# Attention 0 of a gated cross-attention block: the softmax sums divide the context in row form instead of in feature-major form

## The chip, the cores and the metric

The kernel runs on one core of one Trainium2 chip. The metric is the device time of one execution in microseconds (us). The names of the engines in the profile: PE is TensorE (PEld are its weight loads), DVE is VectorE, ACT is ScalarE, POOL is GpSimd, SP is SyncE, which here issues nearly all DMA transfers. SBUF is the on-chip memory, PSUM the matmul results' memory in 8 banks.

## The reference

The block adds four residual parts to x (8 batches of 100 tokens of 512 features); the change is in the first.

```python
x = x + jnp.tanh(g_xattn[0]) * _L0_xattn_ref(_layernorm(x, axis=-1), ctx_1024, ctx_1024, mask, Wq, bq, Wk, bk, Wv, bv)
x = x + jnp.tanh(g_ffn[0]) * _L0_ffn_ref(_layernorm(x, axis=-1), ...)
x = x + jnp.tanh(g_xattn[1]) * _L1_xattn_ref(_layernorm(x, axis=-1), ctx_1024, ctx_1024, ..., Wo, bo)
x = x + jnp.tanh(g_ffn[1]) * _L1_ffn_ref(_layernorm(x, axis=-1), ...)
```

Attention 0 has 16 heads of 32 features over 722 keys per batch:

```python
q = _heads(x_q @ Wq.T + bq)
k = _heads(x_k @ Wk.T + bk)
v = _heads(x_v @ Wv.T + bv)
scores = jnp.einsum('bhqw,bhkw->bhqk', q, k) / np.sqrt(W).astype(np.float32)
scores = scores - 10000.0 * (1.0 - m)
p = jax.nn.softmax(scores, axis=-1)
h = jnp.einsum('bhqk,bhkw->bhqw', p, v)
```

Since the weights of a softmax add up to one, the bias of V may be added after the division by the sums.

## The kernel before

Every engine has its own instruction stream, written out by hand, and engines wait for one another by semaphores. Large products are done as three products of rounded halves (high times high, high times low, low times high), so most tiles exist as a pair h and l (`cxh`, `cxl`, `wkh`, ...).

An attention runs over 64 **pairs** of heads (8 batches, 8 pairs each, loop variable `i`, batch `b = i // 8`). In pair i TensorE computes the scores of pair i+1 (L926 to L931), turns the exponentials of pair i with an identity matrix (L942), does one or two **jobs**, which project keys (L864) or values (L868) of the next batch, and multiplies pair i-1's weights with V (`weigh`, L964; in the last batch L957). ScalarE does the exponentials (L1955) and the high halves, VectorE the maxima (`peak`, L1386), the low halves of the turned weights (`low_turned`, L1392), the gathering of the context (`low_weighed`, L1407 and L1411, in the last batch L1402) and the low halves of the jobs (`low_job`, L1366 for keys, L1370 for values).

The results of jobs, of `weigh` and of the steps below go to two PSUM banks in turn, the **ring**. The list `RINGS` gives the order, and `ring_free(item)` makes TensorE wait until the item two places earlier has been read: `v_job` for a job (DVE's low half), `v_fin` for a `weigh` (the context gathered), `v_sc` for "inv", `v_x0` for "res". So a late VectorE reaches TensorE through these four.

After the 8 pairs of batch b the context stands feature-major in `QT` (512 features x 100 tokens), not yet divided. Then, in pairs of the next batch:

- near i%8 = 2: `inverse` (DVE, L1420) takes the reciprocals `rr` of the sums (100 x 16), `spread_sums` (POOL, L2341) copies each to 32 columns of `rx` (100 x 512);
- i%8 = 4 (`scaled_at`; pairs 12, 20, ..., 60): `turn_sums` (PE, L973, four transposes) turns `rx`, `scale_out` (DVE, L1429) multiplies `QT` with it, `add_bias` (ACT, L1988, four activations) adds the V bias as a column;
- i%8 = 6 (`out_at`; pairs 14, 22, ..., 54, and 61): `turn_out` (PE, L993, four transposes) turns `QT` to rows, `add_out` (DVE, L1492) adds it times tanh(g) to x, which SP has loaded to `x0`. Its semaphore is `v_x0`. Statistics, root and normalized rows follow for the first feed-forward part.

Batch 7 does the same behind the last pair: there the bias is added as a row (`row`, L2567 and L2570 on POOL), and TensorE goes on with the products of the feed-forward part's units 0 and 1 (`inputs`, L1237) in between. VectorE takes a pair's `low_weighed` ahead of its maxima in pairs marked `early`.

## Time and profile before

| | |
|---|---|
| timed runs, median of 3 | 1575.21 us (1574.67 to 1576.0) |
| span of the profiled execution, first to last instruction | 1573.8 us |
| median of the timed runs less that span | 1.4 us |
| PE busy | 1562.0 us, 99% |
| DVE, ACT, POOL busy | 65%, 62%, 27% |
| granted TensorE clock | 1.000 |

The profile is of one execution; its own whole time isn't recorded apart from its span. Attention 0's pairs lie between about 60 us and 485 us, the first feed-forward part follows up to about 1005 us, then attention 1 and the second feed-forward part. Times on the trace are us from the span's start. A bracket at the end of a row, as [0.26 <-ACT V L1921], says how long the engine stood idle before it and who ended that.

### The profile page before, as it was taken

To read this page: it belongs to the slowest core of one execution; us is meant where nothing else is said; L and a number is where in the kernel's file an instruction comes from.
4 is the path that set the end of the run, shared out by engine and by line. 5 is a ranking of instruction groups with operands and counts; after the bars stand their busy time and mean duration, and the time that the engine had idled before them with its cause. 6 is when DMAs were issued, how large, how long until landed. Compare 5 with 4: busy or idle time off the path is not lost.

```text
span 1573.8 us, 25733 instructions
## 1 busy us (share of the span) xinstructions
PE 1562.0 (99%) x9306; PEld 1428.1 (91%) x9306; DVE 1025.1 (65%) x1814; ACT 972.5 (62%) x2014; POOL 426.0 (27%) x570
## 2 busy tenths in 40 slices
PE   9999999999999999999999999999999999999999
PEld 7999899999989999999999998889999989988765
DVE  6577887787786562123644425637777777778987
ACT  5676777677775455444544435447677767767676
POOL 4221222222145222222322222311211121123741
PEclk9999999999999999999999999999999999999999
DMA  8766767687582225554365642576676677658500
GB/s 246 190 169 167 200 179 198 160 206 182 137 220 98 95 81 201 185 180 165 106 230 192 214 165 93 179 181 184 160 193 175 169 189 179 171 142 225 193 13 31
DMA packets 149974, 261.29 MB, mean 166 GB/s; under 512 B 41136, under 2 KB 94000, under 8 KB 149709
## 3 DMA queue, kind: packets, MB, share of 16 engines
q1 hardware_dynamic: 149505, 259.24, 58.8%
q8 instruction: 85, 1.39, 0.4%
q14 instruction: 52, 0.43, 0.1%
q10 hardware_dynamic: 332, 0.23, 0.1%
HBM read 191.01 MB, written 58.57 MB: 159 GB/s over the span
## 4 chain that ended last, share of the span: by engine, by line
PE 94%; DVE 3%; ACT 2%; issue 1%; DMA 0%; ACTq 0%; DVEq 0%
PE ps L1237 33%; PE ps L864 16%; PE ps L868 14%; PE ps L964 8%; PE ps L942 8%; PE ps L1171 2%; PE ps L1033 2%; PE ps L884 2%; PE ps L931 2%; PE ps L926 2%; PE ps L1188 1%; PE ps L929 1%; PE ps L930 1%; ACT P L1955 1%; PE ps L1082 1%
## 5 line engine op out<-in xcount | busy, mean ns | idle before, releaser
L1237 PE MATMUL ps<-ah_f,wh_f 128*128 128x400 f32 x1288 | 442.0, 344 | 0.0
L1237 PE MATMUL ps<-al_f,wh_f 128*128 128x400 f32 x1288 | 441.3, 343 | 0.0
L2319 POOL TENSOR_TENSOR cxl<-raw,cxh 128x384 fp32r<-128x384 f32 (+1 forms) x112 | 105.7, 965 | 556.9 <-ACT cxh L1897 556.9
L1819 DVE TENSOR_TENSOR wl_f<-raw_f,wh_f 128x1024 fp32r<-128x1024 f32 x85 | 103.7, 1223 | 232.2 <-POOL wh_f L2309 232.2
L1386 DVE TENSOR_REDUCE nmax<-ps 100x1 f32<-100x722 f32 x256 | 220.8, 903 | 33.2 <-PE ps L930 29.6
L1237 PEld LDWEIGHTS ps<-al_f,wh_f 128*128 128x128 f32 x1288 | 242.2, 188 | 0.0
L1237 PEld LDWEIGHTS ps<-ah_f,wh_f 128*128 128x128 f32 x1288 | 241.9, 188 | 0.1
L1955 ACT ACTIVATE P<-ps,nmax 100x722 f32<-100x722 f32 x256 | 220.4, 864 | 27.4 <-DVE nmax L1386 27.2
L1967 ACT ACTIVATE PT<-ps 128x400 fp32r<-128x400 f32 x384 | 165.9, 505 | 70.3 <-PE ps L942 69.2
L2237 ACT ACTIVATE raw_f<-wl_f 128x1024 f32<-128x1024 f32 x88 | 93.4, 1062 | 173.7 <-DVE wl_f L1819 173.6
L1392 DVE TENSOR_TENSOR PT<-ps,PT 128x400 fp32r<-128x400 f32 x384 | 196.3, 566 | 3.2
L2309 POOL CAST wh_f<-raw_f 128x1024 fp32r<-128x1024 f32 x85 | 92.8, 1092 | 334.0 <-PE ps L1237 328.3
L864 PE MATMUL ps<-cxh,wkh 128*128 128x338 f32 (+1 forms) x512 | 174.9, 342 | 0.7 <-DVE cxl L1356 0.7
L864 PE MATMUL ps<-cxh,wkl 128*128 128x338 f32 (+1 forms) x512 | 168.4, 329 | 0.0
L864 PE MATMUL ps<-cxl,wkh 128*128 128x338 f32 (+1 forms) x512 | 167.5, 327 | 0.0
L942 PE MATMUL ps<-ident,P 100*128 100x100 f32 (+1 forms) x1536 | 152.9, 249 | 0.7 <-ACT P L1955 0.7
L942 PEld LDWEIGHTS ps<-ident,P 100*128 100x128 f32 (+1 forms) x1536 | 143.1, 137 | 11.1 <-ACT P L1955 0.9
L964 PE MATMUL ps<-PT,V 128*128 128x400 f32 x720 | 152.1, 346 | 0.6 <-DVE QT L1411 0.6
L964 PEld LDWEIGHTS ps<-PT,V 128*128 128x128 f32 x720 | 129.7, 188 | 7.1 <-DVE V L1378 3.7
L1366 DVE SCALAR_TENSOR_TENSOR ksl<-ps,cols,ksh 128x338 fp32r<-128x338 f32 (+1 forms) x120 | 70.8, 590 | 95.9 <-ACT ksh L1908 95.9
L868 PE MATMUL ps<-wvh,cxh 128*128 128x512 f32 x320 | 131.7, 411 | 0.9 <-DVE V L1366 0.9
L868 PE MATMUL ps<-wvh,cxl 128*128 128x512 f32 x320 | 126.0, 394 | 0.0
(227 smaller groups left out, 2669.0 us busy)
## 6 DMA issues: line engine op xcount, KB each, us to landing
KS<-kd SPq DMA_DIRECT2D x192, 361.0 KB
raw_f<-in_h SPq DMA_DIRECT2D x64, 512.0 KB, 4.2
raw_f<-in_gud SPq DMA_DIRECT2D x48, 512.0 KB, 4.3
raw<-in_ctx SPq DMA_DIRECT2D x64, 192.0 KB, 3.5
raw_f<-in_w SPq DMA_DIRECT2D x24, 512.0 KB, 3.5
kd<-ksh SPq DMA_DIRECT2D x60, 192.0 KB, 2.2
kd<-ksl SPq DMA_DIRECT2D x60, 192.0 KB, 2.5
raw<-in_ctx SPq DMA_DIRECT2D x64, 169.0 KB, 4.4
```

The costliest lines, as they stand in the source:

```text
L864: ins = e.matmul(o, m.wk[x][:, k, 128 * j[2]:128 * j[2] + 128], m.cx[y][:, k, off:off + n], start=(k == 0 and c == 0), stop=(k == 3 and c ...
L868: ins = e.matmul(o, m.cx[y][:, k, 128 * kt:128 * kt + KM[kt]], m.wv[x][:, k, :], start=(k == 0 and c == 0), stop=(k == 3 and c == 2))
L942: ins = e.transpose(ps[0:KM[kt], bank, o:o + S], m.P[0:S, (2 * i + h) % 3, 128 * kt:128 * kt + KM[kt]], ident[0:S, 0:S])
L964: ins = e.matmul(o, m.V[b % 2][0:r, kt, g, 128 * pr:128 * pr + 128], m.PT[0:r, i % 2, :, kt, :], start=(kt == 0), stop=(kt == KT - 1))
L1237: return e.matmul(o, p, q, start=start, stop=stop)
L1386: e.tensor_reduce(m.nmax[0:S, c:c + 1], scores_of(n), AX.X, ALU.max, negate=True).then_inc(v_max, 1)
L1392: e.tensor_tensor(lo, ps[:, bank, 0:400].rearrange("p (k n) -> p k n", k=2), raw32(hi), ALU.subtract).then_inc(v_t, 1)
L1819: e.tensor_tensor(wl[:, z, :], raw[:, r, :], raw32(wh[:, z, :]), ALU.subtract).then_inc(v_ul, 1)
L1955: e.activation(m.P[0:S, n % 3, :], scores_of(n), ACT.Exp, bias=m.nmax[0:S, c:c + 1], accum_out=m.rs[0:S, r:r + 1]).then_inc(a_exp, 1)
L1967: e.activation(m.PT[:, i % 2, 0, 2 * x:2 * x + 2, :], ps[:, bank, 0:400].rearrange("p (k n) -> p k n", k=2), ACT.Copy).then_inc(a_t, 1)
L2237: e.activation(raw[:, r, :], raw32(wl[:, z, :]), ACT.Abs, accum_out=low[:, z, 0:1]).then_inc(a_raw, 1)
L2319: e.tensor_tensor(m.cx[1][:, k, off:off + n], m.raw[:, k, off:off + n], raw32(m.cx[0][:, k, off:off + n]), ALU.subtract).then_inc(g_cx, 1)
```

## The change

In attention 0 alone the reciprocal sums are no longer spread, turned and multiplied into `QT`. The undivided context is turned to rows, and VectorE multiplies the rows in their PSUM bank with the reciprocals `rr`, 100 x 16 read with stride 0 over 32 columns; behind a wait for its own result the old L1492 follows. The V bias is loaded once as a row in pair 4, multiplied by tanh(g) on POOL in pair 8, and added to each batch's x rows by POOL (`add_row`) before DVE's sum. The "inv" items leave ring 0, and pairs 12, 20, ..., 60 are no longer `early`.

```diff
-        if scaled_at(_i) is not None:
+        if _l and scaled_at(_i) is not None:
             RINGS[_l].append(("inv", scaled_at(_i)))
...
-        row = at("row", PLACE[0]["Qs"], [128, D])[0:S, :]
+        row = rooms[0].rx[0:S, :, :].rearrange("p h j -> p (h j)")
...
-                        w.wait_ge(d_qs[1], qs_done(L, B - 1))
+                    if L == 0 and i == 4:
+                        w.wait_ge(d_row, 16 * 6)
                         e.dma_start(row, t["bv0"].partition_broadcast(S)).then_inc(d_row, 16)
...
                 def turn_out(b):
-                    if b < B - 1:
-                        w.wait_ge(a_fin, 4 * b + 4)
-                    else:
-                        w.wait_ge(v_sc, B)
+                    w.wait_ge(v_fin, 16 * b + 16)
+                    if summed(L, 8 * b + 7):
+                        w.wait_ge(a_pv, 8 * b + 8)
...
-                    turn_sums(B - 1)
                     add_low()
                     turn_normal(KEPT)
-                    inputs(0, 0, HN, 0, g_xf, 4, [0])
                     turn_out(B - 1)
-                    inputs(0, 0, HN, 0, g_xf, 4, [1])
+                    inputs(0, 0, HN, 0, g_xf, 4)
...
                 def add_out(b):
                     w.wait_ge(a_g, 1)
-                    w.wait_ge(d_x, 16 * (b + 1))
+                    w.wait_ge(g_row, b + 1)
                     w.wait_ge(p_res, b + 1)
+                    w.wait_ge(v_inv, b + 1)
                     x = rows_in(b)
+                    o = ps[0:S, ring_bank(L, ("res", b)), :].rearrange("p (h j) -> p h j", h=H)
+                    me.then(e.tensor_tensor(o, o, m.rr[0:S, :].unsqueeze(2).to_broadcast([S, H, W]), ALU.mult))
+                    me.settle()
                     e.scalar_tensor_tensor(x, ps[0:S, ring_bank(L, ("res", b)), :], G["x0"][0:S], x, ALU.mult,
                                            ALU.add).then_inc(v_x0, 1)
...
-                    if scaled_at(i) is not None:
+                    if L and scaled_at(i) is not None:
                         add_bias(scaled_at(i))
...
+                def add_row(b):
+                    w.wait_ge(d_x, 16 * (b + 1))
+                    e.tensor_tensor(rows_in(b), rows_in(b), row, ALU.add).then_inc(g_row, 1)
...
-                    if scaled_at(i + 1) is not None:
+                    if L and scaled_at(i + 1) is not None:
                         spread_sums(scaled_at(i + 1))
+                    if L == 0 and i == 8:
+                        w.wait_ge(d_row, 16 * 7)
+                        w.wait_ge(a_g, 1)
+                        me.then(e.tensor_scalar(row, row, G["x0"][0:S], None, ALU.mult))
+                        me.settle()
+                    if L == 0 and out_at(i + 1) is not None:
+                        add_row(out_at(i + 1))
```

On TensorE in pair 12, between the turned exponentials (L942) and the first key job, and at the start of the second job (`wkh`, 128x384), the difference reads so; in brackets the semaphores that an instruction waits for:

```order
-L973 MATMUL ps<-ident,rx_54 128x100 [waits v_job,g_rx]
-L973 MATMUL ps<-ident,rx_54 128x100 x3
-L864 MATMUL ps<-cxh_49,wkh_58 128x338 [waits g_cx,v_fin]
+L864 MATMUL ps<-cxh_49,wkh_58 128x338 [waits g_cx,v_job]
...
-L864 MATMUL ps<-cxh_49,wkh_58 128x384 [waits v_sc]
+L864 MATMUL ps<-cxh_49,wkh_58 128x384 [waits v_fin]
```

The four transposes are gone, and the second job waits for the gathered context of pair 10 instead of for `scale_out`.

On VectorE the same pairs 14 and 15 (from `add_out` to the value job of pair 15) read so in the changed kernel; its lines are L1492 for the new product, L1494 for the old sum, L1389 for `low_turned`, L1367 for a value job's low half, L1383 for the maxima, L1404 and L1408 for the gathering:

```order
L1492 TENSOR_TENSOR ps<-ps,rr_55 100x512 [waits v_inv,p_res,g_row]
L1494 SCALAR_TENSOR_TENSOR x_108<-ps,gt,x_108 100x512 [waits v_self]
L1389 TENSOR_TENSOR PT_64<-ps,PT_64 128x2x200 [waits a_t] x3
L1367 TENSOR_TENSOR V_0_61<-ps,V_0_61 128x4x128 [waits a_job]
L1499 BN_STATS st<-x_108 100x6 [waits v_x0]
L1501 BN_AGGR mv<-st 100x2 [waits v_self]
L1383 TENSOR_REDUCE nmax_57<-ps 100x1 [waits a_exp,p_sc] x2
L1404 TENSOR_TENSOR sum_65<-ps,sum_65 64x200 [waits a_pv]
L1408 TENSOR_TENSOR QT_68<-ps,sum_65 32x100 [waits v_self]
L1408 TENSOR_TENSOR QT_68<-ps,sum_65 32x100
L1389 TENSOR_TENSOR PT_64<-ps,PT_64 128x2x200 [waits a_t] x3
L1367 TENSOR_TENSOR V_0_61<-ps,V_0_61 128x4x128 [waits a_job]
```

Before, the first two rows were the single L1492, with waits for `p_res` and `d_x`, and the other ten stood in the same order. In pair 12 VectorE has lost L1429 and does the two maxima ahead of the gathering, which stood before them.

## Rows read from the trace of the kernel before

**Rows 1.** The page: busy time of the engines, and the chain by engine

```profile
PE 1562.0 (99%) x9306; PEld 1428.1 (91%) x9306; DVE 1025.1 (65%) x1814; ACT 972.5 (62%) x2014; POOL 426.0 (27%) x570
...
PE 94%; DVE 3%; ACT 2%; issue 1%; DMA 0%; ACTq 0%; DVEq 0%
```

**Rows 2.** Waits of PE, 80 to 485 us: total, times, longest

```profile
PE ps L929 <- ACT P L1955: 1.3, 4, 0.4
...
```

**Rows 3.** Timeline of PE, pair 12, then pair 56: start, duration, what

```profile
142.46 1.20 PE L942 MATMUL ps<-ident,P 100*128 100x100 f32 x12
143.49 0.51 PE L973 MATMUL ps<-ident,rx 100*128 100x100 f32 x4
143.78 0.40 PE L864 MATMUL ps<-cxh,wkh 128*128 128x338 f32 x1
...
449.96 1.19 PE L942 MATMUL ps<-ident,P 100*128 100x100 f32 x12
450.93 0.40 PE L864 MATMUL ps<-cxh,wkh 128*128 128x338 f32 x1
```

**Rows 4.** The chain in order of time: key jobs of pairs 12 and 13

```profile
144.00 4.11 PE ps L864 x24
150.88 4.00 PE ps L864 x24
```

**Rows 5.** Timeline, pair 12: DVE's scale_out, PE's weight loads of both jobs

```profile
145.10 0.57 DVE L1429 TENSOR_TENSOR QT<-ps,QT 128x400 f32<-128x400 f32 x1
...
145.43 0.19 PEld L864 LDWEIGHTS ps<-cxh,wkl 128*128 128x128 f32 x1
145.73 0.19 PEld L864 LDWEIGHTS ps<-cxh,wkh 128*128 128x128 f32 x1
```

**Rows 6.** Timeline, pairs 14 and 15: DVE, and the weight load behind them

```profile
159.12 0.75 DVE L1492 SCALAR_TENSOR_TENSOR x<-ps,gt,x 100x512 f32<-100x512 f32 x1
...
161.57 0.69 DVE L1370 TENSOR_TENSOR V<-ps,V 128x512 fp32r<-128x512 f32 x1 [0.26 <-ACT V L1921]
162.18 0.68 DVE L1497 BATCH_NORM_STATS2 st<-x 100x6 f32<-100x512 f32 x1
...
167.17 0.69 DVE L1370 TENSOR_TENSOR V<-ps,V 128x512 fp32r<-128x512 f32 x1
...
168.03 1.07 PEld L964 LDWEIGHTS ps<-PT,V 128*128 128x128 f32 x6
```

**Rows 7.** Timeline of DVE, pair 12: two operations with a wait for itself between

```profile
142.37 0.36 DVE L1407 TENSOR_TENSOR sum<-ps,sum 64x200 f32<-64x200 f32 x1 [0.22 <-ACT sum L1982]
142.76 0.55 DVE L1411 TENSOR_TENSOR QT<-ps,sum 32x100 f32<-32x100 f32 x2
```

**Rows 8.** Timeline, pairs 60 to 62: ACT, PE, DVE

```profile
471.43 1.18 ACT L1988 ACTIVATE QT<-QT,cols 128x100 f32<-128x100 f32 x4
...
472.91 1.30 ACT L1967 ACTIVATE PT<-ps 128x400 fp32r<-128x400 f32 x3
...
472.12 1.19 PE L942 MATMUL ps<-ident,P 100*128 100x100 f32 x12
...
473.86 0.75 DVE L1492 SCALAR_TENSOR_TENSOR x<-ps,gt,x 100x512 f32<-100x512 f32 x1
...
476.42 1.73 DVE L1386 TENSOR_REDUCE nmax<-ps 100x1 f32<-100x722 f32 x2 [0.36 <-PE ps L930]
...
478.18 0.87 ACT L1955 ACTIVATE P<-ps,nmax 100x722 f32<-100x722 f32 x1
```

**Rows 9.** Timeline, end of attention 0: PE and DVE

```profile
484.49 0.51 PE L973 MATMUL ps<-ident,rx 100*128 100x100 f32 x4
...
484.92 0.19 PE L982 MATMUL ps<-low_f,magic 128*1 128x3 f32 x2
...
483.82 0.79 DVE L1520 TENSOR_SCALAR x<-x,mv,rq 100x512 f32<-100x512 f32 x1 [0.51 <-POOL rq L2424]
```

**Rows 10.** The line L2570: durations in ns, least, median, most

```profile
L2570 POOL TENSOR_TENSOR x<-x,row x1: 1300/1300/1300, 486.1 to 486.1; 100x512 f32<-100x512 f32 x1
```

More of the change, by code:

```diff
@@ L178 @@
             RINGS[_l].append(("pv", _i - 1))
-for _l in range(2):
-    RINGS[_l].append(("inv", B - 1))
+RINGS[1].append(("inv", B - 1))
 RINGS[0] += [("res", B - 1), ("xn", B - 1)]
@@ L898, in ring_free @@
                     elif old[0] == "inv":
-                        w.wait_ge(v_sc, B * L + old[1] + 1)
+                        w.wait_ge(v_sc, old[1] + 1)
                     elif old[0] == "out":
@@ L981, in add_low @@
                     w.wait_ge(v_const, 4)
[L982 removed]
+                    e.matmul(ps[0:1, 4, 400:403], magic[:, 2:3], low[:, 0:3, 0], start=True,
                              stop=True).then_inc(p_low, 1)
                 def turn_out(b):
[L987 to L990 removed]
+                    w.wait_ge(v_fin, 16 * b + 16)
+                    if summed(L, 8 * b + 7):
+                        w.wait_ge(a_pv, 8 * b + 8)
                     ring_free(("res", b))
@@ L1179, in down @@
                     w.wait_ge(d_wb[4 + q], 16)
-                    w.wait_ge(v_sc, 2 * B)
+                    w.wait_ge(v_sc, B)
                     if n == TILES - 2:
@@ L1417, in inverse @@
                     w.wait_ge(a_exp, LAST * L + 16 * b + 16)
-                    w.wait_ge(g_rx, B * L + b)
+                    if L:
+                        w.wait_ge(g_rx, b)
+                    else:
+                        w.wait_ge(v_x0, b)
                     z = b % 2
@@ L1433, in copy_low @@
                     w.wait_ge(p_low, 1)
-                    e.tensor_copy(low[0:1, 0:3, 1], ps[0:1, ring_bank(L, ("inv", B - 1)), 400:403]).then_inc(v_low, 1)
+                    e.tensor_copy(low[0:1, 0:3, 1], ps[0:1, 4, 400:403]).then_inc(v_low, 1)
                 def add_projected(n):
@@ L1648, in attention @@
                 for i in range(NP + 1):
-                    early = scaled_at(i) is not None or L == 0 and i < NP - 7 and (
+                    early = L and scaled_at(i) is not None or L == 0 and i < NP - 7 and (
                         out_at(i) is not None or turned_at(i) is not None) or L == 0 and NP - 7 < i < NP - 2
@@ L1675, in attention @@
                         add_out(out_at(i))
-                    if scaled_at(i) is not None:
+                    if L and scaled_at(i) is not None:
                         scale_out(scaled_at(i))
@@ L1708, in attention @@
                     copy_low()
-                    scale_out(B - 1)
                     low_normal(KEPT)
-                    w.wait_ge(g_row, 1)
                     add_out(B - 1)
@@ L1984, in add_bias @@
                 def add_bias(b):
-                    w.wait_ge(v_sc, B * L + b + 1)
+                    w.wait_ge(v_sc, b + 1)
                     for g in range(4):
@@ L2139, in attention @@
                         high_q(b + 1)
-                    if scaled_at(i) is not None:
+                    if L and scaled_at(i) is not None:
                         add_bias(scaled_at(i))
@@ L2562, in attention @@
                         tile_roots(2)
-                spread_sums(B - 1)
                 if L == 0:
-                    w.wait_ge(d_row, 16 * 7)
-                    w.wait_ge(a_g, 1)
-                    me.then(e.tensor_scalar(row, row, G["x0"][0:S], None, ALU.mult))
-                    me.settle()
-                    w.wait_ge(d_x, 16 * B)
-                    e.tensor_tensor(x7, x7, row, ALU.add).then_inc(g_row, 1)
+                    add_row(B - 1)
                     high_unit(3)
```

12 lines of the change are left out of this document (5 added, 7 removed).

## The prediction

> **What bounds the kernel now.** I read the page first: TensorE is busy 99% of the span and holds 94% of the chain that ended last [rows 1]. So only what TensorE does less, or waits more or less for, counts. Its waits over attention 0 [rows 2] show the second thing: in 405 us its scores are held by exponentials four times, 1.3 us in all, and these fall in the last batch, which has no projection jobs to fill TensorE. So there are two regimes: batches 1 to 6 of the pair loop, bound by TensorE, where VectorE and ScalarE matter only where their slack ends, and the last batch, bound by the loop scores, maxima, exponentials, turning. ScalarE's bias and POOL's spreading lie beside TensorE's work in the first.
>
> **What is taken off TensorE.** In pair 12 the turned exponentials start at 142.46 and the first key job at 143.78, so 1.32 us later; in pair 56, where no L973 stands between, it is 450.93 - 449.96 = 0.97 [rows 3]. Four transposes cost 0.35 us, not the 0.51 of their row, which counts pipelined ends. Six batches (pairs 12 to 52) are in the first regime: 6 x 0.35 = 2.1 us.
>
> There is a second gain in the same pair. The second key job's first weight load starts at 145.73, 0.06 after `scale_out` ends (145.10 + 0.57), while the load before it came at 145.43 and loads there follow each other by about 0.16: so it was held by `v_sc`, some 0.14 late [rows 5]. The price is in the chain: the 24 key products of pair 12 took 4.11 us, those of pair 13 4.00 [rows 4], and all six batches repeat that (0.09 to 0.11). The changed job waits for pair 10's context instead. VectorE now gathers it behind its two maxima: these can take the gathering's place at about 142.4 [rows 7] and last 1.7 (1.73 in [rows 8]); the gathering adds 0.39 + 0.55 [rows 7], so it is ready near 145.1, while the job, with 0.35 less before it, loads near 145.43 + 0.16 - 0.35 = 145.24. That is close, but in time. Gain 0.10 a batch, so 0.45 with the transposes.
>
> **What is added to VectorE, and how it reaches TensorE.** The new product over 100x512 in PSUM has no row. The nearest is L1370, a tensor_tensor from PSUM over 512 columns, 0.69 us [rows 6]; reading `rr` with stride 0 I price at nothing, writing to PSUM in place of SBUF too. Then comes the wait for its own result: L1411 starts 0.39 after an L1407 of 0.36 [rows 7], so 0.03 on top, and I take 0.72 to 0.73 in all. The bounds: below 0.61, the start-to-start time behind L1370 with no wait (162.18 - 161.57, [rows 6]); above 1.30, POOL's own sum over the same 100x512 [rows 10], far off and on another engine. I take the near row.
>
> Where does this lateness go? In pair 14 VectorE goes straight from `add_out` (159.12) through `low_turned` to the value job's low half at 161.57, where it had stood idle for 0.26 [rows 6]. So 0.47 of the 0.73 remain. From there to the low half of pair 15's value job at 167.17 no row of VectorE has an idle bracket, so that starts near 167.64 and ends at 168.33. Who waits for it? By the ring, `weigh` of pair 14 takes the bank of that job, two places earlier, and its first weight load was issued at 168.03, when the old end, 167.86, was just past [rows 6]. With 0.06 for the semaphore [rows 5] the load now comes at 168.39, 0.36 late. Of a late load TensorE's queue absorbs a little: in pair 12 0.14 late cost 0.10. So 0.36 less 0.05, about 0.31 us per batch. The other two places on that road, `weigh` of pair 13 behind `v_x0` and pair 15's key job behind `v_fin`, come late by less than this, and lateness at an earlier place isn't paid twice.
>
> Net per batch: -0.35 - 0.10 + 0.31 = -0.14; six batches -0.84 us. The TensorE saving is nearly given back by a VectorE that had 0.1 us of slack.
>
> Here a rule of the Trainium skill can be weighed. The rows show that without a wait the next operation starts 0.08 before the end of the 0.69 us one, and with a wait for itself 0.03 behind the end [rows 6, 7], so the wait costs about 0.11. The Trainium skill, "VectorE: DVE Perf Modes", section "The DRAIN you can't avoid", says that a semaphore after each operation costs nothing extra. By it the product would take 0.61, the stall 0.19 instead of 0.31, and the six batches would give -1.56 instead of -0.84. The trace doesn't agree with the rule for these short operations, and I go by the trace.
>
> **Pairs 60 to 64.** ScalarE is on the loop here. L1988's four activations (1.18 from 471.43) stood in front of L1967 at 472.91; without them it can follow TensorE's L942 (472.12 plus a third of its 1.19, and a little) at about 472.66: -0.25 [rows 8]. L973 of pair 60 is free, since TensorE waits behind it. But one pair on, `add_out` of batch 6 stands between the maxima and `low_turned`: +0.73 against an idle time of 0.36, so the maxima of pair 62 start at 476.79 and end at 478.52, and the exponential that started at 478.18 starts 0.34 later, the 0.25 already spent [rows 8]. The rest of the loop, the statistics of batch 6 and POOL's root, on which normalized rows at 483.82 wait [rows 9], all move by that 0.34.
>
> At the very end L973 goes, which holds TensorE from 484.49 to 484.92 [rows 9], 0.43, but the transposes of `turn_out` now stand ahead of the products of unit 0 and wait for the last gathered context, on VectorE behind the normalized rows (483.82 + 0.79 + 0.34 = 484.95, [rows 9]); before, products covered that. Unhindered, TensorE would stand there at about 484.92 + 0.34 - 0.43 = 484.83 plus 0.4 for the four transposes of the normalized rows, so at 485.2; the context is gathered by 484.95 + 0.26 and some 0.2 of semaphores, 485.4 (0.26 an estimate from the halves of L1411, [rows 7]). That exposes 0.2. Sum of the tail: +0.34 - 0.43 + 0.2 = +0.1, with bounds of -0.4 (nothing late) and +0.6 (a dear product).
>
> **Edits at nothing.** POOL is busy 27% [rows 1]: eight sums of 1.30 for eight copies, in pairs where it waits for ScalarE; without that cover the sum stands ahead of its context splits. The x rows are loaded two pairs ahead. In pair 60 the sum stands ahead of two weight splits and may bring the root of batch 6 some tenths late, which I count within the 0.34 above. SP's one load only moves from pair 58 to pair 4. Behind 500 us nothing changes.
>
> **Sum.** 1573.8 - 0.84 + 0.1 = 1573.1 for the span; the median of the runs shown is 1.4 above it, so 1574.5 us.
>
> **The rivals.** *The stalls stay hidden* (17%): the value job's low half can slip because the load at 168.03 didn't really need it, or the product is cheap. Then all six 0.45 and the tail's 0.4 stay: -3.1, 1572.1 us. For it speaks that no row shows TensorE waiting there; against it that the old end was only 0.17 before the load. *The product is dear* (12%), the other side: reading and writing one bank costs VectorE 1.30. The stall per batch becomes 0.92, net +0.47, six times +2.8, and the tail adds 0.6: 1578.6 us. It decides from a product of 0.83 on, where 0.45 is used up; past 1.25 the loss can be measured. *The wait is free*, the page's rule worked out as a mechanism of these rows (8%): -1.56 and +0.1, 1573.7 us. *The moved gathering is late* (5%): pair 12's second job finds `v_fin` later than its load near 145.25, each 0.1 late costs 0.1, six times; with 0.3 late -0.84 becomes +0.96, so 1576.3 us. The forecast has 58%.
>
> **Chances and range.** A measurement of this kernel can tell about 0.2%, 3.15 us, from no change. Beyond it on the fast side lies half of the first rival, 8%; on the slow side most of the second, 9%; the rest, 83%, is within. The range 1572.2 to 1576.8 takes in most of the first rival, the third and fourth, and leaves out the dear product.
>
> **What the changed profile would show.** L973 with 32 products fewer, no L1429 and L1988 before 500 us. The product's own row near 0.69, L1494 0.72 behind its start. Key products of pair 12 at 4.00 in the chain. The weight load of `weigh` in pair 15 directly behind the value job's low half, about 0.06 after its end, six times; if it follows the last key load in step instead, the first rival holds. The distance from pair 12 to pair 20 on TensorE shorter by 0.14. Between 475 and 479 us VectorE without an idle bracket. Wrong would make it: a product of over 0.83, or a wait of TensorE at a job or turning that I counted as in time.

## The result, and the profile of the changed kernel

The change made the kernel slower: 1581.0 us (median of 5 runs, 1580.7 to 1585.6) against 1574.9 us (5 runs, 1574.7 to 1576.0), a ratio of 1.0046 with a 95% interval of 1.0034 to 1.0057. The quotient of the two medians is 1.0039; the ratio is larger, and two of the five runs lie at 1583.9 and 1585.6. The profiled execution spans 1579.0 us, where before's spanned 1573.8. That lies outside the range of the forecast.

The page, busy time and chain, as in [rows 1]:

```profile
PE 1560.1 (99%) x9274; PEld 1425.2 (90%) x9274; DVE 1026.0 (65%) x1814; ACT 965.1 (61%) x1986; POOL 428.6 (27%) x569
PE 93%; DVE 3%; DMA 2%; POOL 1%; ACT 1%; issue 1%; SPq 0%; DVEq 0%; ACTq 0%
```

TensorE has its 32 products fewer and 1.9 us less work, and yet the span is longer. The new thing in the chain is DMA, 2%. The waits of PE, 60 to 500 us, beside [rows 2] (engine, line, what it waited for: us in total, times, longest):

```profile
PE ps L942 <- ACT P L1955: 2.4, 1, 2.4
PE ps L1007 <- DVE x L1522: 2.2, 1, 2.2
PE ps L942 <- DVE PT L1389: 1.6, 1, 1.6
PE ps L929 <- ACT P L1955: 1.0, 3, 0.4
PE ps L957 <- DVE QT L1408: 0.8, 1, 0.8
```

Before, beside the row in [rows 2]:

```profile
PE ps L942 <- ACT P L1955: 0.7, 1, 0.7
PE ps L957 <- DVE QT L1411: 0.4, 1, 0.4
```

Three waits, 6.2 us in all, each once, stand where only 0.7 us stood. The timeline shows where: all are in the last two pairs of batch 7 and behind them.

```profile
476.53 1.52 PE L942 MATMUL ps<-ident,P 100*128 100x100 f32 x12 [1.57 <-DVE PT L1389]
...
482.09 2.26 PE L942 MATMUL ps<-ident,P 100*128 100x100 f32 x12 [2.36 <-ACT P L1955]
484.05 4.18 PE L957 MATMUL ps<-PT,V 128*64 128x200 f32 x36
488.16 0.19 PE L982 MATMUL ps<-low_f,magic 128*1 128x3 f32 x2
490.56 0.57 PE L1007 MATMUL ps<-ident,x 100*128 100x100 f32 x4 [2.22 <-DVE x L1522]
...
491.32 0.43 PE L1234 MATMUL ps<-ah_f,wh_f 128*128 128x400 f32 x1
```

Following them back leads to POOL, which executes in order. Its timeline (in brackets the idle time ahead of a row and what ended it):

```profile
461.31 1.04 POOL L2463 CAST wh_f<-raw_f 128x1024 fp32r<-128x1024 f32 x1 [8.27 <-DMA raw_f<-in_w]
...
466.93 1.04 POOL L2457 TENSOR_TENSOR al_f<-QT,ah_f 128x400 fp32r<-128x400 f32 x1
473.20 1.28 POOL L2346 TENSOR_TENSOR x<-x,rx 100x512 f32<-100x512 f32 x1 [5.23 <-DMA x<-in_x]
474.43 1.03 POOL L2463 CAST wh_f<-raw_f 128x1024 fp32r<-128x1024 f32 x1
475.54 2.36 POOL L2465 TENSOR_TENSOR wl_f<-raw_f,wh_f 128x1024 fp32r<-128x1024 f32 x1
...
486.14 0.23 POOL L2417 TENSOR_SCALAR rq<-mv 100x1 f32<-100x1 f32 x1
```

At 467.97 POOL comes to `add_row` of batch 6 and stands there for 5.23 us, because the x rows have not landed. Before, the same load was awaited by VectorE alone, at 473.86 [rows 8], with no visible wait. Now the split of weight tile 1 (L2463, L2465) stands behind it, and the root of batch 6 behind that. The same two in before's timeline of POOL:

```profile
468.80 1.04 POOL L2458 CAST wh_f<-raw_f 128x1024 fp32r<-128x1024 f32 x1
...
480.90 0.22 POOL L2412 TENSOR_SCALAR rq<-mv 100x1 f32<-100x1 f32 x1 [0.39 <-DVE mv L1499]
```

The other seven of POOL's eight sums found their rows landed: none has a bracket in the timeline. The chain, in order of time, has the load itself:

```profile
462.43 10.70 DMA x<-in_x
473.20 1.28 POOL x L2346
```

10.70 us for 200 KB. Two weight tiles of 512 KB each were requested from 461.48 on, and the load right behind them, 0.95 us later. The other engines, ACT and DVE:

```profile
477.93 1.06 ACT L2237 ACTIVATE raw_f<-wl_f 128x1024 f32<-128x1024 f32 x1 [3.68 <-POOL wl_f L2465]
...
474.51 0.70 DVE L1492 TENSOR_TENSOR ps<-ps,rr 100x512 f32<-100x512 f32 x1 [2.10 <-POOL x L2346]
...
489.05 1.46 DVE L1522 TENSOR_SCALAR x<-x,mv,rq 100x512 f32<-100x512 f32 x1 [2.12 <-POOL rq L2429]
```

So one wait reaches TensorE three times: through VectorE's late product (1.57), through ScalarE, which sums the magnitudes of the late weight tile's low half (L2237) ahead of its exponentials (2.36), and through the late root (2.22).

There is a further loss that no wait shows. Twelve turnings and the products behind them took 1.03 us and 3.43 us start to start before (from L942 over L957 to L973 at 484.49 [rows 9]):

```profile
480.03 1.25 PE L942 MATMUL ps<-ident,P 100*128 100x100 f32 x12 [0.72 <-ACT P L1955]
481.06 3.59 PE L957 MATMUL ps<-PT,V 128*64 128x200 f32 x36
```

Now they take 484.05 - 482.09 = 1.96 and 488.16 - 484.05 = 4.11, so 1.6 us more. The windows, with the granted clock in the third column from the end, then DMA's share and GB/s:

```profile
460.00:465.00 5.00, 4.70 (x47) 4.17 (x45) 4.50 (x10) 4.14 (x10) 3.61 (x3) 1.00 1.04 287
465.00:470.00 5.00, 4.50 (x40) 3.60 (x37) 4.30 (x9) 5.00 (x14) 2.80 (x4) 1.00 1.02 293
...
480.00:485.00 5.00, 2.91 (x18) 2.92 (x19) 3.78 (x10) 3.90 (x10) 4.77 (x5) 0.70 0.00 0
```

Behind idle TensorE the granted clock was 0.70 on average over these 5 us, where before it was 1.00. In windows of 1 us it is 0.52, 0.50 and 0.50 from 482 to 485 and 0.78 in the next: the lower level, 1.2 GHz, for some 3.4 us behind the wait of 2.36, and 2.4 GHz again. And from 455 on all sixteen DMA engines were busy (1.02 to 1.04): the load joined a full queue. In before's windows the share there is the same 1.03 to 1.05.

From `weigh` ahead of pair 57 (L964 at 451.09, before 452.89) to the first product of unit 0 (491.32, before 485.39 and 0.35 for the four L993 that then stood behind it) it is 40.2 us against 32.9, so 7.4 more. The three waits give 6.2 less the 0.7 that before waited for exponentials there, a longer wait of L957 0.4, the clock 1.6, and L973 is gone, -0.4: 7.1 together, within a few tenths of it. The batches ahead had won 1.6 us. The two together make 5.8, and the spans differ by 5.2; the other 0.6 lies outside these two stretches, 0.2 of it ahead of the first scores.

### The profile page after: what moved, and what is told of

Read it like the earlier page. It is cut to its first block, busy times and chain, and to the rows that moved or that the text cites. A ratio compares the mean times of both kernels' runs of the same rounds, so it can differ in the third digit from the quotient of the medians.

```text
span 1579.0 us, 25608 instructions
## 1 busy us (share of the span) xinstructions
PE 1560.1 (99%) x9274; PEld 1425.2 (90%) x9274; DVE 1026.0 (65%) x1814; ACT 965.1 (61%) x1986; POOL 428.6 (27%) x569
## 4 chain that ended last, share of the span: by engine, by line
PE 93%; DVE 3%; DMA 2%; POOL 1%; ACT 1%; issue 1%; SPq 0%; DVEq 0%; ACTq 0%
PE ps L1234 33%; PE ps L864 16%; PE ps L868 14%; PE ps L964 8%; PE ps L942 8%; PE ps L1168 2%; PE ps L1032 2%; PE ps L884 2%; PE ps L931 2%; PE ps L926 2%; PE ps L1185 1%; PE ps L930 1%; PE ps L929 1%; DMA x<-in_x 1%; DMA kd<-ksl 1%
## 5 line engine op out<-in xcount | busy, mean ns | idle before, releaser
L1383 DVE TENSOR_REDUCE nmax<-ps 100x1 f32<-100x722 f32 x256 | 220.8, 904 | 35.8 <-PE ps L930 32.9
L2237 ACT ACTIVATE raw_f<-wl_f 128x1024 f32<-128x1024 f32 x88 | 93.4, 1062 | 177.2 <-DVE wl_f L1819 173.5
L1389 DVE TENSOR_TENSOR PT<-ps,PT 128x400 fp32r<-128x400 f32 x384 | 196.8, 568 | 4.9 <-ACT PT L1967 1.5
L942 PE MATMUL ps<-ident,P 100*128 100x100 f32 (+1 forms) x1536 | 154.2, 250 | 3.9 <-ACT P L1955 2.4
L942 PEld LDWEIGHTS ps<-ident,P 100*128 100x128 f32 (+1 forms) x1536 | 143.9, 138 | 14.8 <-ACT P L1955 2.6
L964 PE MATMUL ps<-PT,V 128*128 128x400 f32 x720 | 152.8, 347 | 0.6 <-DVE QT L1408 0.6
L964 PEld LDWEIGHTS ps<-PT,V 128*128 128x128 f32 x720 | 129.0, 188 | 8.9 <-DVE V L1375 3.7
```

The source lines that it names most:

```text
L942: ins = e.transpose(ps[0:KM[kt], bank, o:o + S], m.P[0:S, (2 * i + h) % 3, 128 * kt:128 * kt + KM[kt]], ident[0:S, 0:S])
L964: ins = e.matmul(o, m.V[b % 2][0:r, kt, g, 128 * pr:128 * pr + 128], m.PT[0:r, i % 2, :, kt, :], start=(kt == 0), stop=(kt == KT - 1))
L1383: e.tensor_reduce(m.nmax[0:S, c:c + 1], scores_of(n), AX.X, ALU.max, negate=True).then_inc(v_max, 1)
L1389: e.tensor_tensor(lo, ps[:, bank, 0:400].rearrange("p (k n) -> p k n", k=2), raw32(hi), ALU.subtract).then_inc(v_t, 1)
L2237: e.activation(raw[:, r, :], raw32(wl[:, z, :]), ACT.Abs, accum_out=low[:, z, 0:1]).then_inc(a_raw, 1)
```

## The experiments

Times are medians of 6 to 11 runs (the change: 5). The ratio is to the kernel before on the same chip, with its 95% interval; before's median was 1574.9 beside the change and 1575.1 to 1575.3 beside the others. The single runs of one kernel spread over 2 to 5 us, so two medians that differ by less than about 1 us are not clear of the noise; where the text reads such a difference, it says so.

| run | us | ratio |
|---|---|---|
| the change | 1581.0 | 1.0046 [1.0034, 1.0057] |
| old_with_wait | 1580.6 | 1.0035 [1.0023, 1.0047] |
| no_row6 | 1575.9 | 1.0003 [0.9994, 1.0013] |
| x6_before_units | 1580.1 | 1.0029 [1.0019, 1.0040] |
| x6_no_product | 1579.4 | 1.0025 [1.0015, 1.0034] |
| x6_before_all | 1580.3 | 1.0030 [1.0019, 1.0041] |
| row7_apart | 1579.4 | 1.0027 [1.0016, 1.0037] |
| row6_behind | 1577.6 | 1.0014 [1.0005, 1.0023] |
| row6_after | 1575.4 | 1.0001 [0.9992, 1.0010] |
| x6_then_units | 1579.6 | 1.0026 [1.0015, 1.0036] |
| mended | 1576.1 | 1.0004 [0.9995, 1.0013] |
| mended_no_product | 1575.2 | 0.9999 [0.9990, 1.0008] |
| old_mended | 1577.1 | 1.0011 [1.0002, 1.0020] |
| mended_one_step | 1575.4 | 1.0003 [0.9994, 1.0012] |
| best | 1575.0 | 1.0000 [0.9991, 1.0009] |
| best_no_product | 1573.4 | 0.9989 [0.9980, 0.9998] |

**The wait alone, in the old kernel.**

```
+                    if L == 0 and i == 60:
+                        w.wait_ge(d_x, 16 * 7)
                     if L == 0 and i in (58, 60, 61):
                         prepare((i - 57) // 2)
```

> The kernel before the change, with a single addition: in pair 60 POOL waits for the transfer of batch 6's x rows before it splits the weights of unit 1. No instruction is added, moved or left out. Theory A: the wait alone reproduces the loss; POOL, which without it starts this split at 468.8 us, starts it near 473.2, and the time is 4 to 6 us above the 1574.9 of before: 1579 to 1581 us. Theory B (the added work, not the wait): within 0.5 us of before, 1574.4 to 1575.4 us.

1580.6 us. POOL waited until the rows landed, as in the changed kernel (timeline of POOL):

```profile
472.31 1.04 POOL L2458 CAST wh_f<-raw_f 128x1024 fp32r<-128x1024 f32 x1 [4.86 <-DMA x<-in_x]
```

A semaphore wait without any work, in a kernel that has none of the change, gives 5.2 of the 6.1 us. So the wait is shown as the cause. The road from POOL to TensorE is in part another one, though (PE):

```profile
487.55 0.56 PE L973 MATMUL ps<-ident,rx 100*128 100x100 f32 x4 [2.94 <-POOL rx L2341]
```

The spread sums of batch 7, late behind the split, hold the old kernel, where the normalized rows hold the changed one. The exponential of pair 63 is late in both (1.73 here, 2.36 there), and the granted clock is 0.50 behind the last wait here too, from 490 to 492.

**The sum of batch 6 left out.** VectorE waits for the rows itself, as before; batch 6 lacks the V bias.

```
-                    if L == 0 and out_at(i + 1) is not None:
+                    if L == 0 and out_at(i + 1) is not None and i < 56:
                         add_row(out_at(i + 1))
```

> The changed kernel without POOL's sum of x and the bias row for batch 6 alone, so that batch 6 lacks its V bias; VectorE waits for the x rows itself, as before the change, and their transfer stays where it is, behind the weight tiles. Theory A (the wait at the head of POOL's queue costs the time): POOL goes straight on to the weight splits, 1573.0 to 1575.5 us, and the difference to the run with the transfer moved is at most 1 us, what the 1.28 us of work cost. Theory C (the late rows would hold VectorE just as long, whoever waits for them): VectorE waits for the transfer until 473.1 in front of its product instead, and the time stays over 1577 us.

1575.9 us, 5.1 under the changed kernel. That is 0.4 above the range of theory A, and far from theory C; the run with the transfer moved, the next one, is not within 1 us of it, as theory A wanted, but 4.2 above. All other steps of the change are in this run, and the forecast's range (1572.2 to 1576.8) holds it. The run takes off the wait and 1.28 us of work together; row6_after below keeps the work. Two rows of its timeline of DVE matter below:

```profile
473.71 0.70 DVE L1495 TENSOR_TENSOR ps<-ps,rr 100x512 f32<-100x512 f32 x1 [0.63 <-DMA x<-in_x]
...
483.96 1.48 DVE L1525 TENSOR_SCALAR x<-x,mv,rq 100x512 f32<-100x512 f32 x1 [0.52 <-POOL rq L2432]
```

**The rows ahead of weight tiles 2 and 3.**

```
                     if L == 0 and i == 58:
+                        load_x0(B - 2)
                         for u in range(2, 4):
                             fetch(("unit", u))
```

> The changed kernel, with one transfer moved: in pair 58 the x rows of batch 6 are requested ahead of the weight tiles of units 2 and 3 (512 KB each) instead of behind them, one pair later. All work is kept, POOL's sum for batch 6 too. Theory A (POOL, which works in order, stands 5.2 us at this sum because the rows land 10.7 us after their request, and the weight splits behind it come late): POOL's wait before the sum goes to under 0.5 us, TensorE's waits of 1.6, 2.4 and 2.2 us in pairs 62 and 63 and at the end of attention 0 shrink to under 1 us in sum, and the time is 1573.5 to 1575.5 us, so 0.995 to 0.997 of the changed kernel's 1581.0. Theory B (POOL is simply overloaded: its eight sums of 1.28 us and the weight splits don't fit before the end of attention 0): the transfer makes no difference, 1580 to 1582 us.

1580.1 us. Theory A as I had put it (the rows are late because of the two tiles just ahead) fails: requested at 460.79, they still land 9.35 us later. The time lies in the range of theory B (POOL overloaded), but B doesn't hold either: old_with_wait loses 5.2 us with no work added, and row6_after below does all eight sums and splits in 1575.4 us. PE and POOL:

```profile
470.20 1.27 POOL L2347 TENSOR_TENSOR x<-x,rx 100x512 f32<-100x512 f32 x1 [2.87 <-DMA x<-in_x]
...
487.66 0.56 PE L1008 MATMUL ps<-ident,x 100*128 100x100 f32 x4 [3.79 <-DVE x L1523]
...
488.98 0.54 PE L1235 MATMUL ps<-ah_f,wh_f 128*128 128x400 f32 x1
```

With 1 MB less ahead the landing took 1.35 us less, which is no more than the spread between kernels of one request order (behind all four tiles 10.1 to 11.6 us in five traces, in this order 9.4 and 10.4 in two); POOL's wait was 2.4 shorter, and the root ended 2.9 us earlier. TensorE's wait for VectorE's product is gone, but it reached the normalized rows the sooner and stood there 3.79 us in one piece. Behind that its products took 0.54 each and not 0.34; ten of them at a distance of 0.33 in place of 0.18 cost some 1.5 us. So a wait halved on POOL gave 0.9, about the noise.

**The same without the product.** The context goes into the sum undivided.

```
-                    me.then(e.tensor_tensor(o, o, m.rr[0:S, :].unsqueeze(2).to_broadcast([S, H, W]), ALU.mult))
-                    me.settle()
```

> The changed kernel with the transfer of batch 6's x rows moved ahead of units 2 and 3, and without the product of the rows with the reciprocal sums and the wait for it, so the context stays undivided. It measures what VectorE's 0.73 us cost the seven batches. If the lateness reaches TensorE as the changed trace shows (0.18 and 0.18 us before weigh in pairs 14 and 15 of six batches), both waits go, pair 12 to pair 20 becomes shorter by another 0.2 us, and the whole is 1.2 to 2.0 us below the run that keeps the product. If VectorE's lateness is hidden, the two are within 0.5 us.

1579.4 us, 0.7 less, between the two ranges that I had written down and within the noise, although TensorE's L965 ahead of pair 57 starts at 449.56 and not at 450.41. POOL still waits 3.2 us. The product isn't the cause.

**The rows ahead of all four weight tiles.**

```
                         w.wait_ge(g_cx, 56)
+                        load_x0(B - 2)
                         for u in range(2):
                             fetch(("unit", u))
```

> The changed kernel, with the x rows of batch 6 requested ahead of all four weight tiles of pairs 57 and 58 (behind the same waits as the first of them); no work is left out. Theory A (the rows land late because they queue behind weight tiles, and GpSimd's in-order sum holds everything behind it): with the rows at the head of the burst the sum waits for nothing. What is left over the run without the sum is the sum itself, 1.28 us less the 0.28 us that GpSimd stood idle there before the root of batch 6: 1576.9 us. Rival B (the loss is in the weight tiles' own landing, and rows put ahead of them only push them back by their 200 KB): 1578 to 1580 us, with GpSimd's wait moved from the sum to the first split of a weight tile.

1580.3 us, where theory A wanted 1576.9. POOL's sum waits for nothing, as expected, but TensorE does (timeline of PE, then the window behind it):

```profile
473.44 0.75 PE L927 MATMUL ps<-KS,QS 98*100 98x512 f32 x1 [3.78 <-DMA KS<-kd]
```

```profile
475.00:480.00 5.00, 5.00 (x31) 4.99 (x30) 3.35 (x6) 4.00 (x8) 4.84 (x5) 0.50 0.00 0
```

The keys of pair 61 now land late, 3.78 us, and TensorE runs the next 5 us at a granted clock of 0.50. Rival B is right that the loss moves, wrong about where to: POOL's first split began at 463.49, yet the wait that counts is that of the keys. The wait was only handed to the next transfer that somebody needs.

**The sum for batch 7 behind the normalized rows**, on top of that kernel.

```
                 if L == 0:
+                    w.wait_ge(v_xn, 8 + KEPT)
                     add_row(B - 1)
```

> The kernel with the rows ahead of all weight tiles, and in it GpSimd's sum for batch 7 waits until VectorE has written the normalized rows of batch 6; no work is left out. In the trace of the run without the sum of batch 6 those normalized rows took 1.48 us beside GpSimd's sum of two inputs, and 0.79 us in the kernel before, where GpSimd copied beside them. Theory C (GpSimd's sum slows VectorE's operation): the operation falls to 0.55 to 0.8 us, the turnings behind it come 0.6 us earlier, and the time is 0.6 us under the kernel with the rows ahead of all tiles, 1576.3 us. If the operation is long for another reason, it stays at 1.4 to 1.5 us and the time at 1576.9 us.

1579.4 us, 0.9 less (0.6 expected), not clear of the noise. What shows is in the trace. The keys' wait is there again, 3.3 us, but the row that this run is about changed (DVE):

```profile
487.66 0.55 DVE L1523 TENSOR_SCALAR x<-x,mv,rq 100x512 f32<-100x512 f32 x1 [0.51 <-POOL rq L2430]
```

0.55 us alone, 0.79 beside POOL's copy [rows 9], 1.46 to 1.48 beside POOL's sum of two inputs. Theory C holds for the operation: `add_row` for batch 7 made it 0.7 to 0.9 us longer, and TensorE waited on it. That the time falls with it is not shown by these two runs. The Trainium skill, "SBUF — State Buffer", section "Who interferes with whom", says that VectorE in a mode that takes both ports (a tensor_scalar such as this one can enter it) and GpSimd block each other for a whole instruction, not in part. These rows agree roughly: POOL's sum ran from 483.87 to 485.15 in the run without the sum of batch 6, and the operation begun at 483.96 ended at 485.44, a little sooner than 0.55 behind it.

**The sum of batch 6 behind the split of weight tile 1.**

```
                         prepare((i - 57) // 2)
+                    if L == 0 and i == 60:
+                        add_row(6)
```

(and `i != 60` at its old place)

> The changed kernel, with GpSimd's sum of batch 6 placed behind its split of weight tile 1 in pair 60 in place of ahead of it; the request of the rows stays where the change has it, and no work is left out. Two things were late in the changed kernel: VectorE's product (2.1 us for the sum) and ScalarE's measurement of the split tile (3.7 us for the split behind the sum). If the second is what cost, the split is in time again, root and exponentials come about 2 us earlier than in the changed kernel, and the time is 1577.5 to 1578.5 us. If VectorE's own wait for the sum is what cost, nothing changes: 1580.5 to 1581.5 us.

1577.6 us, just within what the first reading wanted. POOL and VectorE still wait for the rows, and VectorE 2.6 us, but ScalarE's wait for the split tile is gone. Of the 6 us lost, 3.4 came not from who waits for the load but from what stood behind it in POOL's queue.

**The bias of batch 6 added afterwards.** VectorE adds context and rows; POOL adds the bias row behind the split of weight tile 2; the root stands ahead of the last split; the sum for batch 7 waits for the normalized rows.

```
                         prepare((i - 57) // 2)
+                    if L == 0 and i == 61:
+                        w.wait_ge(v_x0, KEPT + 1)
+                        add_row(KEPT)
...
                         split_kept(4)
+                        batch_root(KEPT)
                         split_kept(5)
-                        batch_root(KEPT)
```

> A version made to beat the change: for batch 6 VectorE adds context and rows without the bias, and GpSimd adds the bias row afterwards, behind its split of weight tile 2, where nothing is waited for; the root of batch 6 stands ahead of GpSimd's last split, and the sum for batch 7 waits for the normalized rows. No work is left out. Theory A: no engine waits for the late rows except VectorE's own sum (0.6 us in the run without the sum on GpSimd), the root is as early as in that run (1575.9 us) and the normalized rows 0.6 us shorter: 1575.3 us. Rival: six batches of attention 0 gain about 1.5 us, but the last batch is bound by data that land from full DMA queues, which start no earlier, so the floor is the kernel before's 1575 us whatever is mended: 1575 to 1576 us as well, but with waits for DMA or for the split tiles in place of the ones removed.

1575.4 us, nothing lost and nothing won, with all the work in it. Both theories allowed this time; the waits for DMA that the rival wanted are there. POOL waits for no load from 463 us on. What is left is (PE, DVE):

```profile
470.97 0.48 PE L928 MATMUL ps<-KS,QS 98*100 98x512 f32 x1 [1.08 <-DMA KS<-kd]
...
474.44 0.70 DVE L1497 TENSOR_TENSOR ps<-ps,rr 100x512 f32<-100x512 f32 x1 [1.03 <-DMA x<-in_x]
```

**Weight tiles 2 and 3 requested when the rows have landed.**

```
-                    if L == 0 and i == 58:
+                    if L == 0 and i == 59:
+                        w.wait_ge(d_x, 16 * 7)
                         for u in range(2, 4):
                             fetch(("unit", u))
```

> The changed kernel, with weight tiles 2 and 3 requested only when the x rows of batch 6 have landed; no work is left out. With the rows ahead of these tiles, but the tiles requested right behind them, the rows still landed 9.4 us after their request. Theory D (requests made later share the DMA engines with those made earlier, so 1 MB right behind the rows delays them as well): the rows land 2 us earlier or more, by about 468 us, GpSimd's sum waits under 0.5 us, the keys of pair 61 aren't late, and the time is that of the run without the sum plus the sum, 1576 to 1577 us. Rival (strict order: what is requested later doesn't matter): the rows land 9 us after the request, GpSimd waits over 2 us, 1579 to 1580 us.

1579.6 us: the rival. Requested at 462.74, awaited until 471.49, 8.7 us with nothing behind them on the queue. Theory D as I had put it falls: the rows don't land 2 us sooner, and POOL waits 2.3 us. That what is requested later costs nothing at all is not shown: in three more traces with the tiles held back (mended, mended_one_step, mended_no_product) the rows took 7.4, 8.5 and 9.2 us, in the two with the tiles right behind 9.4 and 10.4. The bulk of the landing is there without them, a delay of a microsecond or so by them stays open. The Trainium skill, "DMA: Bandwidth & Descriptors", section "Queues, rings and completion order", has each DMA engine take its descriptors in ring order, and this pair of runs agrees within that spread. TensorE's wait for the normalized rows was 3.76 us, with the clock down behind it (0.50 in every microsecond from 488 to 494). The profiled run was the slowest of eight, 1582.4 us.

**That kernel, mended** by the root ahead of the last split and the sum for batch 7 behind the normalized rows.

```
                         split_kept(4)
+                        batch_root(KEPT)
                         split_kept(5)
-                        batch_root(KEPT)
```

> The kernel with weight tiles 2 and 3 requested when the x rows have landed, with two edits more: the root of batch 6 stands ahead of GpSimd's last split, and GpSimd's sum for batch 7 waits until the normalized rows of batch 6 are written (this took their 1.48 us to 0.55 us). No work is left out. By theory D all the changed kernel's new waits are gone and the gain of the six batches, some 1.5 us in the trace, shows at last: 1573.5 to 1575 us. If the floor is the loop scores, maxima, exponentials of the last batch with VectorE's product in it, the time is 1575 to 1576 us, with no wait for DMA left in the trace.

1576.1 us, in neither range: above the first, and with a wait for DMA left, which the second excluded (POOL and PE):

```profile
470.43 1.27 POOL L2347 TENSOR_TENSOR x<-x,rx 100x512 f32<-100x512 f32 x1 [0.97 <-DMA x<-in_x]
...
485.53 0.56 PE L1008 MATMUL ps<-ident,x 100*128 100x100 f32 x4 [1.08 <-DVE x L1523]
```

> The kernel before this one without VectorE's product and the wait for its result in attention 0: the context goes into the sum undivided. It prices the product and its wait as a whole with the last batch free of DMA waits. By the steps of the prediction it is 6 x 0.31 + 0.34 = 2.2 us; the traces of the two runs with late rows gave 0.23 per batch, so 1.4 us plus 0.3 to 0.7 in the last batch. Expected: 1.7 to 2.2 us under the kernel with the product. If the last batch is bound by landing data and not by VectorE, less than 1 us.

Its edit is the one of x6_no_product. 1575.2 us, 0.9 less, half of what I expected, and what I had written down for a last batch that is bound by landing data. TensorE waited 1.99 us for an exponential at 478.61, and the pair behind it ran at a low clock (window 480 to 485 us: 0.66); the time won ahead was waited away there.

> The kernel before the change with the same request order (weight tiles 2 and 3 when the x rows have landed) and with the root of batch 6 ahead of GpSimd's last split; no work is left out. It tells whether the mended change beats the kernel before for its own sake or only by the mending. The kernel before has no visible wait for either: expected within 0.7 us of 1575.2 us. If the old kernel too was held by crowded DMA queues, it gains 1 us or more, 1573.5 to 1574.2 us.

1577.1 us: the same request order and the same place of the root, in the kernel before, lose 2 us. The row that says why (PE):

```profile
485.37 0.56 PE L975 MATMUL ps<-ident,rx 100*128 100x100 f32 x4 [1.36 <-POOL rx L2343]
```

The old kernel's `spread_sums` stands behind the last split on POOL, and the root ahead of it pushes it back. Behind this wait TensorE's clock was down as well:

```profile
485.00:490.00 5.00, 4.63 (x24) 4.33 (x25) 1.50 (x4) 0.51 (x1) 4.16 (x4) 0.70 0.00 0
```

In windows of 1 us it is 0.50 from 487 to 490. POOL's order there fits one kernel at a time. I had not looked at what stood behind.

**Three runs on what holds the last batch.** `best` is row6_after with the rows requested ahead of weight tiles 2 and 3 (the edit of x6_before_units).

> The version with the bias of batch 6 added behind GpSimd's split of weight tile 2, and with the x rows of batch 6 requested ahead of weight tiles 2 and 3; no work is left out. In its first form VectorE waited 1.0 us for the rows, which cost TensorE 0.5, and TensorE waited 1.1 us for the keys of pair 61. Theory E (the last batch is held by what lands from the full DMA queues, piece by piece): the wait for the rows goes, the keys still come late: 1574.7 to 1575.1 us. Rival F (the last batch is held by GpSimd's unbroken chain from the landing of weight tile 0 to the root of batch 6): earlier rows change nothing, 1575.4 us.

1575.0 us, 0.5 less than row6_after and in theory E's range, but the difference is within the noise. VectorE's wait for the rows is gone, the keys' is not:

```profile
470.86 0.48 PE L929 MATMUL ps<-KS,QS 98*100 98x512 f32 x1 [1.32 <-DMA KS<-kd]
```

> The version before this one without VectorE's product and the wait for its result in attention 0: the context goes into the sum undivided. Theory E or F: the six batches end about 1.4 us earlier, the last batch begins earlier too, but waits for the landed data and for GpSimd until the same moment, so that 0.3 to 1.0 us remain of it. If instead VectorE's product is what holds the last batch, over 1.7 us remain.

1573.4 us, 1.6 less, clear of the noise, more than theory E or F allowed and close to the bound for the product itself. With POOL and the rows out of the way, most of what the product costs shows at the end.

`mended_one_step` takes one Newton step out of the root of batch 6:

```
-                    for step in range(2):
+                    for step in range(b == KEPT, 2):
```

> The kernel with weight tiles 2 and 3 requested when the x rows have landed, the root of batch 6 ahead of the last split and the sum for batch 7 behind the normalized rows (1576.1 us), with one Newton step in place of two in that root, which takes three of GpSimd's small operations off, 1.0 us from start to start in its trace; the root is a little less exact. Rival F: TensorE waited 1.1 us for the normalized rows there, so the root is on the path that sets the end, and the time falls by 0.8 to 1.0 us, to 1575.2 us. Theory E alone (landings): under 0.3 us.

1575.4 us, by the medians 0.75 less for three small operations of POOL, nearly what rival F wanted; by the means it is 0.3 less, which theory E allowed. The spread of the two kernels (1574.5 to 1577.0 and 1574.4 to 1577.1) doesn't decide it. In the traces TensorE's wait for the normalized rows fell from 1.08 to 0.44, while the one for the exponential ahead of it rose from 1.23 to 1.49. What the three runs show together is less than I had wanted to know: in the last batch waits of about a microsecond for landing keys, for exponentials and for POOL's root stand one behind the other, and which of them sets the end is open; only the product's 1.6 us is clear.

## Why the prediction was wrong

**The step that failed** is in the edits counted at nothing: "The x rows are loaded two pairs ahead." For batch 6 that held for VectorE alone, which adds in pair 61 what SP requests in pair 59. POOL's sum stands in pair 60, one pair behind the request: it was reached 5.5 us after it (462.43 to 467.97), and the load took 10.7. In [rows 8] VectorE's L1492 began at 473.86 in the very moment in which its maxima had ended, and I took the absence of a wait for slack. Nothing said how early the rows had landed: only a wait or its absence is seen. With POOL as the new consumer, needing them at 468 and not at 473.9, the load was 5.2 us late, a wait that the sum of the prediction had at nothing. "That the sum may bring the root of batch 6 some tenths late" was mis-sized by the same step: the root began at 486.14 and not at 480.90. None of the rivals held it, and the one on the slow side, a dear product, gave 1578.6 for another reason.

The working could have seen it, by an estimate from the trace of before. From 452.39 to the request of the rows at 463.13 SP had requested six loads of keys of 361 KB, two stores of 169 KB, four weight tiles of 512 KB and the bias row of 200 KB; with the rows themselves that is 5.1 MB. Its windows show full engines from 455 to 470 us at 260 to 294 GB/s, so 17 to 19 us for all of it: the rows could not be counted on before about 470, and POOL would ask for them at 468.

**What held.**

- *The sum as a whole, without that step*: 1575.9 (no_row6), 1575.4 (row6_after), 1575.0 (best) against 1574.5 forecast.
- *Transposes and key job*: in the changed kernel's chain the key products of pair 12 take 4.00 us (4.11 in [rows 4]), and the first follows the turning at 143.22 - 142.25 = 0.97 us.
- *The product, 0.72 to 0.73 with its wait*: 0.70, and L1494 starts 0.73 to 0.74 behind it. So writing to PSUM in place costs nothing that shows, and the wait for itself is 0.03 again, not free. Timeline of DVE, pairs 14 and 15:

```profile
158.45 0.70 DVE L1492 TENSOR_TENSOR ps<-ps,rr 100x512 f32<-100x512 f32 x1
159.18 0.75 DVE L1494 SCALAR_TENSOR_TENSOR x<-ps,gt,x 100x512 f32<-100x512 f32 x1
...
161.30 0.68 DVE L1367 TENSOR_TENSOR V<-ps,V 128x512 fp32r<-128x512 f32 x1
...
166.88 0.68 DVE L1367 TENSOR_TENSOR V<-ps,V 128x512 fp32r<-128x512 f32 x1
```

- *The road of the lateness*: the idle time of 0.26 ahead of the value job's low half is gone, and the weight load of `weigh` in pair 15 follows the low half of that pair by 0.05, as forecast. But the road has a second place: the weight load of `weigh` in pair 14 waits for the old sum. The prediction had named it and counted it as not paid (PEld):

```profile
159.99 1.02 PEld L964 LDWEIGHTS ps<-PT,V 128*128 128x128 f32 x6 [0.19 <-DVE x L1494]
...
167.61 1.02 PEld L964 LDWEIGHTS ps<-PT,V 128*128 128x128 f32 x6 [0.21 <-DVE V L1367]
```

- *The size, -0.84 for six batches*, lies in what the traces give. From the first scores (L926 at 59.20 before) to L964 ahead of pair 57 it is 393.7 us in before, and the same in the two other traces of the old kernel, and 392.1 in after; ten more traces with the product give 392.1 to 393.1, so -0.6 to -1.6. Without the product three traces give 391.0 to 392.2, so -1.5 to -2.7, where the steps had -2.7. The product's stall is then roughly 0.2 per batch, and I had 0.31.
- *The tail's +0.1* was too kind even without the failed step: no_row6 comes to its last scores 0.7 us ahead of before (L929 at 462.69 for 463.41) and leaves at 486.25 where before left at 485.39 + 0.35. Of that 1.2, the exponential of pair 62 is late (1.24 of waiting for 0.72), and the transposes of the normalized rows waited 0.6, since L1525 took 1.48 for 0.79. That `add_row` for batch 7 slows VectorE was in no step.

Still open is why 200 KB ahead of everything (x6_before_all, row7_apart) brought the keys 3.3 to 3.8 us late, when the same 200 KB behind them left between nothing and 1.4 of it. Weight tile 0 landed later too (POOL's first split at 463.4 and 463.5 for 460.6 to 462.8 in the other traces of the changed kernel). I have no run that separates it.

## What to carry to other kernels

A load's consumer that does not wait tells you nothing of when the load landed. Before a load gets an earlier consumer, price its landing from what is queued ahead of it and from DMA's share in the windows; 200 KB took 10.7 us here. A wait on an in-order engine costs what stands behind it, not what it is for: moving one sum behind one split gave back 3.4 of 6 us. And microseconds won ahead of a stage that waits for landings and for a side engine's chain can be waited away in it: of the 0.6 to 1.6 us that the six batches won, no version with all the work showed more than 0.2 against before at the end.

## What the runs showed of the hardware

- With the DMA engines full from 455 to about 470 us, a 200 KB load landed 7.4 to 11.6 us after its request: 10.1 to 11.6 behind four weight tiles (five traces), 9.4 and 10.4 with the last two tiles (1 MB) requested behind it, 7.4 to 9.2 with these held back until it had landed (four traces). The kernels differ in more than the order, so the steps between these groups are estimates, not prices.
- TensorE's clock: behind single waits of 2.9 to 3.8 us (old_with_wait, x6_before_all, row7_apart, x6_before_units, x6_then_units) a window of 5 us at or next to the wait shows a granted clock of 0.50 to 0.79, and products of 128x400 took 0.54 in place of 0.34. Of the seven waits of 2.0 to 2.4 us three were followed by it (0.70 in the changed kernel at 482, 0.66 in mended_no_product and in x6_no_product at 480), four not (2.22 in the changed kernel at 490, 2.12 in row6_behind, 2.26 in x6_before_units at 479, 2.22 in x6_no_product at 488). Behind waits of 1.1 to 1.7 us the windows stay at 1.00 with one exception, a wait of 1.36 us (old_mended, at 485), behind which it fell to 0.70. So the length of the last wait alone doesn't tell whether the clock falls; where it fell, it was 0.50 for 3 to 7 us.
- The same VectorE operation over 100x512 took 0.55 us alone, 0.70 beside GpSimd's cast of 128x400 (mended, row6_after), 0.79 beside its copy and 1.46 to 1.48 beside its sum of two inputs.
